# A feed-forward stage on eight cores: the next tile's first products pulled in front of the last quantisation, with a third buffer for the hidden activations

## The reference, cut to what matters

```
x = x + attn(layernorm(x))          # stage A, not touched by the change
x = x + ffn(layernorm(x))           # stage B

def fp4_linear(x, w):               # x and w rounded to an FP4 grid in blocks of 16
    return einsum('bsk,nk->bsn', fp4_quant_dequant(x), fp4_quant_dequant(w))
def ffn(x):
    gate = fp4_linear(x, w_gate)    # 1024 -> 2816
    y    = fp4_linear(x, w_up)      # 1024 -> 2816
    h    = silu(gate) * y
    return fp4_linear(h, w_down)    # 2816 -> 1024, h is quantised first
```

## Time and profile before

| | |
|---|---|
| device time, median of 3 runs | 8148.66 us (8144.37 to 8154.72) |
| the profiled execution's own time | 8152.19 us |
| its span (slowest core, 7) | 8150.6 us |
| spans of all cores | 8118.1 to 8150.6 us |
| DVE busy | 5104.1 us, 63% |
| PE busy | 4463.0 us, 55% |
| ACT busy | 2039.9 us, 25% |
| mean granted TensorE clock, core 7 | 0.722 of full speed |

### The profile page before, as it was taken

The page is one execution under the profiler, slowest core; times in us unless marked ns, Lnnn a source line. Parts: engine busy times, 40 slices in busy tenths (PEclk is TensorE's granted clock), DMA queues, the critical chain, the costliest instruction groups (busy, mean ns, idle before and its releaser), DMA issues.

```text
span 8150.6 us, 63704 instructions; the slowest of 8 cores (8118.1 to 8150.6 us)
## 1 busy us (share of the span) xinstructions
PE 4463.0 (55%) x17096; PEld 1792.6 (22%) x17096; DVE 5104.1 (63%) x9316; ACT 2039.9 (25%) x2835; POOL 368.6 (5%) x464
## 2 busy tenths in 40 slices
PE   3466666666665660355555555555555555555555
PEld 1122222222222220122222222222222222222222
DVE  2455556556555563467666766766676676667666
ACT  0133333333333330122222222222222222222222
POOL 0000000000000000000000000000000000000000
PEclk8666667767776675677777777777777777777777
DMA  2111111111111113100000000000000000000000
GB/s 58 42 46 43 39 44 45 39 43 45 39 45 41 38 47 81 35 11 16 16 13 14 16 16 11 16 16 11 15 16 16 11 16 16 11 16 16 16 11 16
DMA packets 131791, 224.37 MB, mean 28 GB/s; under 512 B 76146, under 2 KB 77170, under 8 KB 131442
## 3 DMA queue, kind: packets, MB, share of 16 engines
q10 hardware_dynamic: 94578, 86.07, 3.7%
q1 hardware_dynamic: 18432, 67.12, 2.8%
q0 software_dynamic: 18432, 67.12, 2.0%
HBM read 118.56 MB, written 84.41 MB: 25 GB/s over the span
## 4 chain that ended last, share of the span: by engine, by line
DVE 48%; PE 17%; ACT 15%; issue 11%; DMA 7%; DVEq 1%; POOL 1%; ACTq 0%; POOLq 0%; SPq 0%
PE psa L769 5%; PE psa L950 4%; PE psa L958 4%; DMA x<-x 3%; DVE lbh L362 3%; DVE bmh L986 3%; ACT lbh L365 2%; DVE lbh L395 2%; DVE lbh L386 2%; DVE lbh L404 2%; DVE lbh L401 2%; DVE lbh L377 1%; DVEq L157 1%; DVE hbP L977 1%; DVE invh L996 1%
## 5 line engine op out<-in xcount | busy, mean ns | idle before, releaser
L1024 PE MATMUL psa<-wdT,hqT 128*128 128x512 f16 x2816 | 918.8, 497 | 1133.4 <-ACT hqT L1017 1128.8
L950 PE MATMUL psa<-wgT,xqT 128*128 128x512 f16 (+1 forms) x3072 | 1180.6, 392 | 420.1 <-ACT xqT L932 420.1
L958 PE MATMUL psa<-wuT,xqT 128*128 128x512 f16 (+1 forms) x3072 | 1172.5, 391 | 0.0
L1024 PEld LDWEIGHTS psa<-wdT,hqT 128*128 128x128 f16 x2816 | 327.4, 121 | 1663.2 <-issue 1539.3
L1012 PE MATMUL pst<-id,hqP 128*128 128x128 f16 x1408 | 338.7, 241 | 585.4 <-DVE hqP L418 404.1
L977 DVE TENSOR_TENSOR hbP<-sil,up 128x512 f16<-128x512 f16 (+1 forms) x384 | 142.4, 399 | 612.1 <-ACT up L974 612.1
L412 ACT ACTIVATE lbh<-hbP 128x1024 f16<-128x1024 f16 (+1 forms) x192 | 189.4, 986 | 1279.2 <-DVE lbh L404 1279.2
L950 PEld LDWEIGHTS psa<-wgT,xqT 128*128 128x128 f16 x3072 | 320.4, 104 | 790.8 <-issue 531.5
L549 PE MATMUL psa<-g_k,xlnT 128*128 128x512 f16 x1024 | 392.6, 473 | 115.2 <-ACT uu L611 77.8
L769 PE MATMUL psa<-a,wT 128*128 128x512 f16 x1024 | 374.0, 545 | 79.9 <-ACT wT L765 79.9
L531 PE MATMUL pst<-id,xln 128*128 128x128 f16 x512 | 135.0, 264 | 484.6 <-DVE xln L520 417.7
(11 more groups left out here) (159 smaller groups left out, 7577.6 us busy)
## 6 DMA issues: line engine op xcount, KB each, us to landing
x<-x SPq DMA_DIRECT2D x64, 512.0 KB, 4.0
x2spill<-x POOLq DMA_DIRECT2D x64, 512.0 KB, 4.8
x<-x2spill SPq DMA_DIRECT2D x64, 512.0 KB, 3.2
out<-x POOLq DMA_DIRECT2D x64, 512.0 KB, 3.0
qraw<-wg ACTq DMA_DIRECT2D x22, 512.0 KB, 3.5
qraw<-wu ACTq DMA_DIRECT2D x22, 512.0 KB, 3.5
qraw<-wd ACTq DMA_DIRECT2D x16, 512.0 KB, 3.6
wgq<-q16b ACTq DMA_DIRECT2D x22, 256.0 KB, 3.8
```

The lines of the kernel that those rows point to most:

```text
L950: t_.matmul(PSA[pj][:, 0:wj], xqT[rr][:, kk * 128:(kk + 1) * 128], WgT[:, kk * DFF + joff: kk * DFF + joff + wj], start=(kk == 0), stop=(k ...
L958: t_.matmul(PSA[pj][:, 512:512 + wj], xqT[rr][:, kk * 128:(kk + 1) * 128], WuT[:, kk * DFF + joff: kk * DFF + joff + wj], start=(kk == 0), ...
L1024: t_.matmul(PSA[2][:, hh * 512:(hh + 1) * 512], hqT[r][:, gk * 128:(gk + 1) * 128], WdT[:, gk * D + hh * 512: gk * D + (hh + 1) * 512], st ...
```

## The change

Tile t's last part is recorded in another order. `emit_xprefix_c` still follows down(1), but the next tile's chunks 0 and 1 (gu0', h0', gu1', h1') now follow it at once and stand ahead of mid(2). Before, mid(2) was recorded ahead of `emit_xprefix_c`, and gu0' to h1' after both. As h0' and h1' now write a pair-0 buffer while pair 2 is not yet quantised, `hbP` gets a third buffer, chosen by the pair's number; `hqP` keeps two.

```diff
-    hbP = [SB2(f"hbP_{m}", [128, 1024], F16) for m in range(2)]
+    hbP = [SB2(f"hbP_{m}", [128, 1024], F16) for m in range(3)]
...
-            m2 = (j // 2) % 2
+            m2 = (j // 2) % 3
...
-            m2 = m % 2
+            m2 = m % 3
+            mq = m % 2
...
-                hqP[m2][:, 0:pw].rearrange("p (b k) -> p b k", k=16), f"hqP_{m2}",
+                hqP[mq][:, 0:pw].rearrange("p (b k) -> p b k", k=16), f"hqP_{mq}",
...
-            if m == 2 and t + 1 < NT:
+            emit_trdown_pair(m)
+            if m == 1 and t + 1 < NT:
+                emit_xprefix_c(rn)
                 emit_gu(0, rn)
                 emit_h(0)
                 emit_gu(1, rn)
                 emit_h(1)
-            emit_trdown_pair(m)
             if 2 * m + 2 < 6:
                 emit_mid_pair(m + 1)
-            if t + 1 < NT:
-                if m == 0:
-                    emit_xprefix_a(rn, f"x2_{rn}")
-                    emit_xprefix_b(rn)
-                elif m == 1:
-                    emit_xprefix_c(rn)
+            if t + 1 < NT and m == 0:
+                emit_xprefix_a(rn, f"x2_{rn}")
+                emit_xprefix_b(rn)
```

## The result

The changed kernel takes 8496.4 us (median of 8 runs, 8462.55 to 8529.42), the kernel before 8153.22 (8 runs). The ratio is 1.0413, with a 95% interval of 1.0389 to 1.0437. The forecast was 8484 us. In some executions the cores of one die are granted a lower clock and take longer; in the profiled one it was 0.707 on core 3, the slowest, and 0.718 on core 7.

What follows compares the result with a forecast made beforehand. The prediction took DVE's in-order queue, with one hole of about 9.5 us per tile, as the bound. It added 63 x 5.3 = 334 us to 8152, giving 8486 against the median 8483, and predicted 8484 us, range 8450 to 8640.

Steps and rivals of the forecast that it cites:

- DVE's queue with one hole is the bound: Stage B: DVE's in-order queue, with one hole of about 9.5 us at h0' and h1', sets a tile's length.
- The copy to `xqT` comes 5.5 us earlier: ACT, ahead of mid(2)'s Abs and Sign: PE's stall falls from 6.87 to about 1.34 us, gu0' comes 5.5 us earlier.
- The products ahead of mid(2) cost more than that: DVE: 13.3 us of mid(2) no longer run beside PE's chain; only 5.5 of stall and 2.35 of slow clock come off.
- The clock: PE at gu0' and gu1': they start at full instead of half clock, 2.35 us less per tile.
- Rival A: At gu0' and gu1': clock falls in PE's short stall, so they start at half clock; 8634 us, chance 0.12.
- the row used: PE, from down(1)'s start to the identity matmuls' start: 5.34 us in the profiled tile that the prediction worked from.
- the sum: DVE's wait for h0' and h1': 14.87 against 9.44 us, a tile 5.43 longer, taken as 5.3; 63 tiles give 334.
- Rival D: The stall gained on ACT and the wait added on DVE cancel: time stays at 8150 us within 0.2%, chance 0.02.
- What follows mid(2) is hidden, by a few tenths: Pair 2's transposes, down(2), gu2', gu3' under DVE's mid(0)': h3' product ready at X + 16.6, DVE there at X + 17.0.
- rival B: Behind mid(2), PE's clock stays low through down(2), gu2', gu3', so h3' comes late: 8902 us, chance 0.04.
- Rival C: Faster: down(1)'s start decides; issued where the transposes end, DVE finds h0' and h1' ready, 7557 us; chance 0.03.

Runs made afterwards that it cites:

- early_copy: Kernel before with gu4 to down(1) recorded before the next tile's layer norm, and identity matmuls and copy to xqT ahead of mid(2): 0.9280 of before.
- early_down1: Kernel before with only gu4 to down(1) recorded ahead of the next tile's layer norm and quantisation: 0.9974 of before.
- copy_first: Kernel before with only the next tile's identity matmuls and copy to xqT moved ahead of mid(2), two hbP buffers: 0.9497 of before.
- early_after: Changed kernel with gu4 to down(1) also recorded before the next tile's layer norm and quantisation: 1.0235 of the kernel before.
- copy_between: Kernel before with the next tile's identity matmuls and copy to xqT placed between mid(2)'s Abs and its Sign: 0.9467 of before.
- copy_first_again: Repeat, for comparison on the same chip, of the kernel before with only identity matmuls and xqT copy ahead of mid(2): 0.9484 of before.

## Why the prediction was right, point by point

**DVE's queue with one hole is the bound.** Right. Closing the hole (early_copy) gave 65.4 us per tile, and moving PE's work alone (early_down1) gave nothing.

**The copy to `xqT` comes 5.5 us earlier.** Right as a fact: PE's wait at L950 is 1.36 where 1.34 was worked out. By itself it is a gain of 5.0% (copy_first), so one half of the changed kernel is a gain.

**The products ahead of mid(2) cost more than that.** Right. It is the step that turns the sign: copy_first and the changed kernel differ only in the place of h0' and h1' against mid(2) on ACT and DVE (PE's order is the same) and in the buffer, and the buffer costs nothing. From 0.9497 to 1.0413 the early products cost 9.2 points.

**The clock.** Right: gu0' starts at full clock, and the 2.35 us come off. Rival A is out on the die with the lower clock too: on core 3 it is 7.1 us on the mean from the start of gu0' to the Silu of h1', where A needed 9.26. What was not uniform is down(1), which starts behind 15 us of idle PE. On core 3 of the changed kernel:

```profile
5021.20 6.61 PE L1025 MATMUL psa<-wdT,hqT 128*128 128x512 f16 x16 [15.28 <-ACT hqT L1018]
5027.64 0.70 PE L926 MATMUL psa<-id,xq 128*128 128x128 f16 x8
```

6.44 us from start to start, where the row used had 5.34. The mean over core 3's rows was 5.52, on core 7 5.38, on core 7 before 5.27.

**Size.** The hole grew by 15.02 - 9.49 = 5.53 us per tile on core 7; the sum had 5.43 and took 5.3. The tile grew by only 5.00. Some 0.4 of the missing 0.5 are hand-overs on DVE that the sum left out. Before, h5 and h1' were each followed by the reduction that reads them, 0.11 and 0.10 us after their end (5062.23 to L986; 5085.83 to 5085.93). Now h1' is followed by mid(2), which starts at 5092.78, 0.08 before h1' ends, and mid(2) by mid(0)', 0.09 before its end:

```profile
5025.54 0.56 DVE L418 TENSOR_TENSOR hqP<-lbh 128x768 f16<-128x768 f16 x1
5026.01 1.21 DVE L987 TENSOR_REDUCE bmh<-hbP 128x64 f32<-128x1024 f16 x1
...
5042.51 0.75 DVE L977 TENSOR_TENSOR hbP<-sil,up 128x512 f16<-128x512 f16 x2
```

These hand-overs, 0.4 us of 80, are what the sum mis-sized. On the slowest core, 3, whose mean clock was 0.707, other terms made up for it: the hole is longer there and the tile grew by 80.67 - 75.05 = 5.6. 63 x 5.6 is 354, against 334 predicted and 8496 - 8153 = 343 measured. That the median lies only 12 us from the forecast is therefore in part luck: in the fastest execution, 8462.55 us, all cores had a clock of 0.717 or more, and the growth was 8462.55 - 8153 = 310. The sum had no term for a clock of 0.81, which the next point shows. Rival D, that gain and loss cancel, is out with an interval that starts at 1.0389.

**What follows mid(2) is hidden, by a few tenths.** Right on core 7, where the two products of h2' and h3' run together at 5042.51. down(2), taken at 4.9 us, took 3.9 to 5.1 from its start to the next matmul. On core 3 the few tenths ran out in 24 of the tiles, 25.1 us in all, as in this one:

```profile
3525.51 1.21 DVE L1062 TENSOR_TENSOR x<-x,psa 128x1024 f32<-128x1024 f32 x1
3526.64 0.42 DVE L977 TENSOR_TENSOR hbP<-sil,up 128x512 f16<-128x512 f16 x1
3527.80 0.42 DVE L977 TENSOR_TENSOR hbP<-sil,up 128x512 f16<-128x512 f16 x1 [0.73 <-ACT up L974]
```

What differed was the clock. The chapter on the kernel before names two levels, 1.00 and 0.50; the rows of core 3 show a third, 0.81, through gu2' and gu3' of this tile:

```profile
3521.00:3523.00 2.00, 2.00 (x10) 0.82 (x8) 1.79 (x3) 0.58 (x1) 0.00 (x0) 0.81 0.00 0
```

In 21 of the 24 tiles the clock was at 0.81 a few microseconds ahead of the wait; on core 7 it never stood there in this execution, and DVE never waited at these products. This is rival B in its smallest form, at 0.81 and not at 0.50; its 750 us needed every tile.

**Rival C was priced wrong.** It said that the start of down(1) decides and that DVE would then lose its whole wait, 7557 us. early_after made that start early and got 8345 on the same scale. The working had looked at one input of the chain only. The identity matmuls need `xq` too, and DVE finishes that just ahead of h0' and h1', so with the products there DVE must wait for a chain that it has itself only just released. The time that rival C named exists, but it takes the other order (early_copy).

What stays open: why down(1) took 6.1 us in copy_between and 5.1 in its neighbour on the mean of core 0, on the same chip. The clock was at 0.50 for longer. In copy_between down(1) starts at 5030.92, and the clock is still low here:

```profile
5035.00:5036.00 1.00, 1.00 (x4) 0.31 (x3) 0.39 (x2) 0.51 (x1) 0.00 (x0) 0.50 0.00 0
```

In copy_first_again it starts at 5030.21, and the clock is up at about the same distance from the start:

```profile
5034.00:5035.00 1.00, 1.00 (x7) 0.45 (x5) 0.00 (x0) 0.00 (x0) 0.00 (x0) 1.00 0.00 0
```

What kept it low was not tried.

## What to carry to other kernels

Where engines execute in order, moving a piece of work ahead moves it ahead in every queue that it uses. Ask for each queue what it now stands in front of, and whether that work was the cover for the wait: here the matmul side wanted to go ahead, and the elementwise side, which was the bound, had to stay. Split such a piece, advance the part that the idle engine waits for (here the identity matmuls and one copy), and leave the part that waits for PE behind the work that covers it. And before a start time is called what decides, list all inputs of the first step.

## What the runs showed of the hardware that was not expected

On core 3 of the changed kernel the granted clock stood at 0.81 through stretches of dense matmuls, as in the row above, while core 7 had no such stretch in the same execution. Two 512-column matmuls took 0.52 us from start to start at 0.81 (3523.47 to 3523.99) and 0.43 at 1.00 (core 0 of copy_first_again, 5037.13 to 5037.56). Two DVE instructions where the second reads what the first wrote stand about 0.1 us apart (5085.83 to 5085.93 before); where it doesn't, the second starts about 0.1 us before the first one's recorded end (5092.78 against 5092.86 after). In a loop of 80 us that changed the sum by 0.4. And a run of 16 matmuls behind 15 us of idle PE took anything from 4.8 to 6.4 us in the same execution on core 3 of the changed kernel; in the two tiles of copy_between and copy_first_again whose clock is shown above, the longer one is the one in which the clock rose later.
